# Moving a graph kernel's table look-ups from the node stage into the first softmax and the weighting stage

## The reference

```python
edge_index = jnp.stack([src, dst])
x = _layernorm(x + _L0_gnn_ref(x, node_vec, edge_weight, edge_attr_128, ...))   # attention over incoming edges
x = _layernorm(x + _L1_gnn_ref(x, ...))                                         # three graph convolutions
x = _layernorm(x + _L2_gnn_ref(x, edge_attr_128, src, dst, ...))                # two message layers
x = _layernorm(x + _L3_gnn_ref(x, edge_attr_2, src, dst, ...))                  # edge attention
```

## Time and profile before

| | us |
|---|---|
| timed runs: median (lowest to highest) of 3 | 3603.18 (3602.86 to 3603.41) |
| the profiled execution's own time | 3606.04 |
| its span, first to last instruction | 3604.0 |
| VectorE busy | 2602.9 (72%) |
| TensorE busy | 2523.9 (70%) |
| GpSimd busy | 2052.6 (57%) |
| ScalarE busy | 2013.2 (56%) |
| granted TensorE clock, mean | 0.86 |

### The profile page before, as it was taken

How to read it: one execution, slowest core, us unless ns; L and a number is a source line. 1 busy time by engine, 2 the same in 40 slices (tenths; PEclk the granted TensorE clock), 3 DMA queues, 4 the chain that set the end, 5 groups by cost and what they waited for, 6 DMA issues and landing times. The chain is left out here.

```text
span 3604.0 us, 57246 instructions
## 1 busy us (share of the span) xinstructions
PE 2523.9 (70%) x14627; PEld 1907.0 (53%) x14627; DVE 2602.9 (72%) x7782; ACT 2013.2 (56%) x5963; POOL 2052.6 (57%) x1978
## 2 busy tenths in 40 slices
PE   5377744999476777697687787777767757877430
PEld 2133322666355565575466666555557757776430
DVE  8689963444597899998366677798868759878542
ACT  0034322777222888798466677688867748865110
POOL 7767774774000433342777577577467767710776
PEclk9799986999799988999899899888889979987555
DMA  3455557776299444432566677677589879933221
GB/s 94 106 147 153 154 151 165 248 243 205 86 328 273 141 147 147 135 92 77 174 212 199 190 244 247 217 239 240 181 252 269 241 237 290 284 121 112 86 89 42
DMA packets 521868, 653.93 MB, mean 181 GB/s; under 512 B 99208, under 2 KB 292294, under 8 KB 521544
## 3 DMA queue, kind: packets, MB, share of 16 engines
q1 hardware_dynamic: 455242, 548.98, 48.8%
q0 software_dynamic: 65856, 100.90, 10.3%
q10 hardware_dynamic: 446, 0.40, 0.0%
HBM read 436.87 MB, written 241.92 MB: 188 GB/s over the span
## 5 line engine op out<-in xcount | busy, mean ns | idle before, releaser
L1620 POOL DMA_INDIRECT look<-table_d,ids x196 | 196.1, 1000 | 603.8 <-DVEq L1596 559.7
L1945 POOL DMA_INDIRECT xg_c<-r_d,src_row x392 | 410.9, 1048 | 167.9 <-issue 117.1
L2703 POOL DMA_INDIRECT out<-x_f,out_row x196 | 202.9, 1035 | 177.3 <-DVE x_f L2769 118.5
L1945 POOL DMA_INDIRECT xg_c<-x1d_d,src_row x196 | 216.8, 1106 | 104.8 <-issue 59.5
L1945 POOL DMA_INDIRECT xg_c<-x2d_d,src_row x196 | 203.5, 1038 | 113.0 <-issue 59.2
L925 POOL DMA_INDIRECT xd<-in_x,ids x196 | 217.6, 1110 | 71.0 <-issue 51.7
L1945 POOL DMA_INDIRECT xg_c<-g1d_d,src_row x196 | 204.7, 1044 | 79.6 <-issue 59.5
L554 POOL DMA_INDIRECT rows_d<-row,slot_i x196 | 194.1, 990 | 69.4 <-issue 55.8
L2059 ACT ACTIVATE term_c<-xg_c,scale 128x128 f32<-128x128 f32 x392 | 125.1, 391 | 181.3 <-DMA xg_c<-x1d_d,src_row 107.6
L1964 DVE TENSOR_TENSOR_SCAN agg_t_c<-flags_c,agg_t_c,term_t_c 128x512 f32<-128x512 bf16 x96 | 122.9, 1281 | 104.7 <-ACT term_t_c L2043 59.9
L1964 DVE TENSOR_TENSOR_SCAN agg_t_c<-flags_c,agg_t_c,t_ps_c 128x512 f32<-128x512 bf16 x144 | 183.2, 1273 | 1.0 <-PE t_ps_c L2366 1.0
(11 more groups left out here) (483 smaller groups left out, 8896.0 us busy)
## 6 DMA issues: line engine op xcount, KB each, us to landing
flags_c<-cont_d SPq DMA_DIRECT2D x245, 128.0 KB, 4.4
xm<-rows_d SPq DMA_DIRECT2D x49, 512.0 KB
m_d<-m_c SPq DMA_DIRECT2D x98, 256.0 KB
r_d<-r_c SPq DMA_DIRECT2D x98, 256.0 KB
m_in_c<-m_d SPq DMA_DIRECT2D x98, 256.0 KB
e_c<-rows_d SPq DMA_DIRECT2D x98, 256.0 KB
x_f<-in_x SPq DMA_DIRECT2D x67, 256.0 KB, 4.9
out<-x_f SPq DMA_DIRECT2D x67, 256.0 KB
```

The lines of the kernel that those rows point to most:

```text
L1620: pool.indirect_dma_start(out=look[:, t, :], out_offset=None, in_=table_d[:, :], in_offset=bass.IndirectOffsetOnAxis(ap=ids[:, 0, t:t + 1] ...
L1945: pool.indirect_dma_start(out=xg[:, s, k, :], out_offset=None, in_=table, in_offset=bass.IndirectOffsetOnAxis(ap=src_row[:, t:t + 1], axis=0),
L2703: pool.indirect_dma_start(out=out[:, :], out_offset=bass.IndirectOffsetOnAxis(ap=out_row[:, t:t + 1], axis=0), in_=x4[:, n % SF, k, :], in ...
```

## The change

The 196 look-ups leave the node stage. A function `look_up(pool, begin, end)` issues the look-ups of tiles begin to end one after the other, with no wait between them, and then waits until all so far have landed. GpSimd gets a part in the first softmax that looks up tiles 0 to 49 (FIRST_LOOKS is 50), and one in the weighting stage for tiles 50 to 195 (146 of them). The semaphore `looked` is taken before the first softmax and given back after the weighting stage. The whole diff:

```diff
--- before.py
+++ after.py
@@ -1116,6 +1116,18 @@
 
 
 
+        looked = signal("looked", 16, "pool_queue")
+        FIRST_LOOKS = 50
+
+        def look_up(pool, begin, end):
+
+            for t in range(begin, end):
+                pool.indirect_dma_start(
+                    out=look[:, t, :], out_offset=None, in_=table_d[:, :],
+                    in_offset=bass.IndirectOffsetOnAxis(ap=ids[:, 0, t:t + 1], axis=0),
+                    bounds_check=TABLE - 1, oob_is_err=False).then_inc(looked.sem, 16)
+            pool.wait_ge(looked.sem, looked.at(end))
+
         with ExitStack() as st:
             given_l = sb("given_l", [ROWS, 3, LONG], F32, st)
             most = sb("most", [ROWS, 3, LONG], F32, st)
@@ -1134,6 +1146,10 @@
                     for v in range(2):
                         sp.dma_start(attn_d[v, :].rearrange("(r l) -> r l", l=LONG), seen[:, v, :]).then_inc(once_out.sem, 16)
                     sp.wait_ge(once_out.sem, once_out.at(2))
+
+                @block.gpsimd
+                def _(pool):
+                    look_up(pool, 0, FIRST_LOOKS)
 
                 @block.tensor
                 def _(pe):
@@ -1226,6 +1242,10 @@
                     for s in range(3):
                         sp.wait_ge(x1_out[s].sem, x1_out[s].at(len(range(s, GROUPS, 3))))
 
+                @block.gpsimd
+                def _(pool):
+                    look_up(pool, FIRST_LOOKS, TILES)
+
                 @block.tensor
                 def _(pe):
                     for n in range(GROUPS):
@@ -1286,7 +1306,7 @@
                             settled(dve)
                             dve.tensor_tensor(x1[:, n % 3, :, :], y_ps[n % 3][:, :].rearrange("p (k d) -> p k d", k=K),
                                               inv[:, n % 2, :].unsqueeze(2).to_broadcast([P, K, D]), ALU.mult).then_inc(x1_ready.sem, 1)
-            retire([(s, GROUPS) for s in (weighted, scanned, made_y, squared, x1_ready)])
+            retire([(s, GROUPS) for s in (weighted, scanned, made_y, squared, x1_ready)] + [(looked, TILES)])
             for s in (spread_ready, rooted):
                 s.spent(GROUPS)
             retire([(g_in[s], 5 * shares(s, SG)) for s in range(SG)] + [(x1_out[s], shares(s, 3)) for s in range(3)])
@@ -1328,7 +1348,6 @@
             shift = sb("shift_n", [P, 2, K], F32, st)
             rest = sb("rest_n", [P, K], F32, st)
             setup = signal("dense_setup")
-            looked = signal("looked", 16, "pool_queue")
             x_in = [signal(f"x_in{s}", 16) for s in range(6)]
             x4_out = [signal(f"x4_out{s}", 16) for s in range(3)]
             s_out = [signal(f"s_out{s}", 16) for s in range(2)]
@@ -1612,17 +1631,6 @@
                         sp.wait_ge(x2_out[s].sem, x2_out[s].at(len(range(s, GROUPS, 2))))
                         sp.wait_ge(g1_out[s].sem, g1_out[s].at(len(range(s, GROUPS, 2))))
 
-                @block.gpsimd
-                def _(pool):
-                    for it in range(1, NG):
-                        pool.wait_ge(spread_ok.sem, spread_ok.at(it))
-                        for t in range(TILES * (it - 1) // (NG - 1), TILES * it // (NG - 1)):
-                            pool.indirect_dma_start(
-                                out=look[:, t, :], out_offset=None, in_=table_d[:, :],
-                                in_offset=bass.IndirectOffsetOnAxis(ap=ids[:, 0, t:t + 1], axis=0),
-                                bounds_check=TABLE - 1, oob_is_err=False).then_inc(looked.sem, 16)
-                    pool.wait_ge(looked.sem, looked.at(TILES))
-
                 @block.tensor
                 def _(pe):
                     for it in range(NG + LAG):
@@ -1644,7 +1652,7 @@
 
             retire([(s, NG) for s in (turned_x, xt_ready, made_1, squared_1, y2_ready, turned_y, yt_ready, squared_2, made_2,
                                       g1_ready, made_3, leaked, halved, summed_2, added_u)])
-            retire([(looked, TILES), (setup, 1), (spread_ok, NG + 7), (rooted_n, NG + 7), (inv_ready, NG + 7), (normed, NN)])
+            retire([(setup, 1), (spread_ok, NG + 7), (rooted_n, NG + 7), (inv_ready, NG + 7), (normed, NN)])
             retire([(s, GROUPS) for s in (sloped_g, x1s_ready, x2s_ready, turned_g, g1o_ready)])
             retire([(x_in[s], len(range(s, NG, 6))) for s in range(6)] + [(x4_out[s], len(range(s, NN, 3))) for s in range(3)])
             retire([(group[s], shares(s, 2)) for group in (s_out, x2_out, g1_out) for s in range(2)])
```

## The result

The kernel after takes **3668.5 us** (median of four runs, 3651.4 to 3675.7) against 3603.3 (3602.9 to 3604.3): ratio **1.0174**, 95% interval 1.0143 to 1.0205. I had predicted slower, 3650.7 us in a range of 3638 to 3679; the time lies inside, 17.8 us above my number.

The account below looks back on a forecast made before the run. Each stage was taken to end with its last engine, GpSimd in both filled stages. Node stage 0, softmax +30.0 and weighting stage +17.5 give +47.5 us: 3603.2 becomes 3650.7 us, 8-in-10 range 3638 to 3679.

Parts of the forecast that it names:

- The edge holds GpSimd: At stage edges: GpSimd enters with the other engines, so look-ups of a stage cannot start in the stage before.
- Rival four: At the edges: GpSimd may run on through them, look-ups start before 927, not slower, 3603 us; chance 0.05.
- The node stage is worth 0: Node stage: taking the look-ups out brings 0 us, bounds 0 and -1, as VectorE and ScalarE cover them.
- The price, and what holds a look-up: Per look-up: 1.00 us plus 0.30 of issue; VectorE instructions with both inputs in SBUF hold it until they end.
- Softmax, +30.0: First softmax: 50 look-ups outlast the old stage end and add 30.0 us, bounds +25.9 to +32.0.
- Weighting stage, +17.5: Weighting stage: 146 look-ups, some held by VectorE, end late and add 17.5 us, bounds 0 and +43.
- what SP's last write took: Both stage ends: 1.9 us from the last look-up's end to the next stage's first issue, taken from SP's write.
- Five look-ups in two rounds: Weighting stage: beside VectorE's rounds of 3.63 us, five look-ups take two rounds, 7.25 us, 1.45 us each.
- DMA 0: Weighting stage: DMA traffic of 146 look-ups, 7.2 us, could delay VectorE but stays under GpSimd's tail; 0 us.
- rival one: Weighting stage: only two look-ups a round, 1.81 us each, +43 us there, 3676 us in all; chance 0.20.
- Two (nothing held): Both stages: no look-up is held, softmax +25.9 and weighting stage 0, 3629 us in all; chance 0.09.
- Three: Weighting stage: VectorE waits for look-ups too, 20 to 69 us in place of 17.5, middle 3678 us; chance 0.06.

Follow-up runs that it names:

- the repeat of before: The kernel before, unchanged, run again with a profile on the same chip: 3604.2 us, its weighting stage 189.3 us.
- the split: Against the kernel before: 24 look-ups in the first softmax, 96 in the weighting stage, 76 in the node stage; 3601.4 us against 3601.3, ratio 0.9997.
- weighting only: The change with only its 146 weighting-stage look-ups moved, the other 50 back in the node stage: 3638.7 us, ratio 1.0098 to the kernel before.

## Why the prediction was right, and where its terms were off

*The edge holds GpSimd*: right. The softmax starts at 927.87, its first look-up at 928.57; the weighting stage at 1000.68 and 1001.40. Rival four is out.

*The node stage is worth 0*: right. 555.5 to 558.5 us in five kernels with 50, 76, 146 or no look-ups in it, 556.3 with all 196; the 561.1 of after's profile came in no other.

*The price, and what holds a look-up*: right, and now shown. Two inputs in SBUF hold it; with one in PSUM none of 146 is held.

*Softmax, +30.0*: measured +31.2. That is luck: two errors nearly cancel. From the stage's start to the last look-up's end I had 69.8 us, it was 66.9: 7 are held, but for 1.4 us in all, where I had 4.2 (996.9 less 992.7). The tail was 5.9 us, not 1.9.

*Weighting stage, +17.5*: measured +26.0 (29 to 33 against the repeat of before). The term that was mis-sized is again "what SP's last write took": 5.0, not 1.9, +3.1. It was taken from another engine's work; in its place stand the last look-up's landing (1.5 and 1.9 us at the two edges) and GpSimd's DRAIN (4.1 and 2.7). The stretch without an issue adds 7.1 and was in no step, though before shows two such in its node stage, hidden there, of 5.25 us ahead of its 35th look-up (1249.68) and 3.15 ahead of its 114th (1479.88). Its DRAIN of 6.8 us was in that trace too. The rest came out 1.8 shorter. 17.5 + 3.1 + 7.1 - 1.8 = 25.9.

*Five look-ups in two rounds*: right in kind. "A scan that lets GpSimd pass is 0.05 us longer" was right for the scan, but I did not ask which of VectorE's other operations the next look-up would meet: two rounds are 7.47 us, not 7.25, worth 0.04 us a look-up. The held one takes 1.96 us, not 1.76.

*DMA 0*: right. VectorE's last x is out at 1197.2, 22 us ahead of the stage's end.

*The rivals.* The median, 3668.5, is nearer to rival one's 3676 than to my 3650.7; that it came out so is the tail and the stretch, not the rival's mechanism. The trace decides against that: two look-ups a round would have been 1.81 us each, they came every 1.46 to 1.49. Two (nothing held) fell with the held ones. Three happened on a small scale: VectorE waits for GpSimd, with its 128x4 operations, 5.0 us in all, under GpSimd's tail. The Trainium skill (SBUF — State Buffer, "Who interferes with whom") lists tensor_scalar, not only operations with two SBUF inputs, among those that can take the pair of ports and then contend, if their operands allow it. The trace agrees in that the TENSOR_SCALAR of 128x4 is held (0.40 us for 0.17), and I had weighed the rule for the scan alone. By this section of the Trainium skill whoever issues first keeps the pair for its whole instruction; the traces differ, since a TENSOR_SCALAR that starts in the first 0.50 us of an indirect DMA isn't held.

*The number.* It lies in the range for reasons that were partly not mine: of the 11.4 us between my +47.5 and the profile's +58.9, the two tails are +7.1, the stretch +7.1, fewer or shorter holds -4.7, and the rest lies outside the two stages. The other 6 us up to the median are differences between runs. What is not explained is the spread, 24 us over the change's first four runs where before had 1.4, though on the later chips before spread by 13 and 20 us too.

## What to carry to other kernels

An idle engine offers room only up to the end of the stage's own last worker. Before moving work under it, fill the stage on paper (first start, spacing beside that neighbour, and the engine's own way out of the stage, 5 to 6 us here) and move only what fits: 24 and 96 look-ups fitted and cost nothing where before takes 3601 us, 50 and 146 cost 65. Count in the way out what grows with the work: GpSimd's DRAIN was 7.9 us behind 96 look-ups. On the two chips where before takes 4286 and 4317 us even what fitted cost 56 to 74 us, so measure on more than one. Take the tail from an edge that the same engine reaches last after the same kind of work, not from whichever edge is near. And where work leaves a place in which it was hidden, expect nothing back.

## What the runs showed of the hardware

- The order of the two starts isn't all. A scan with two SBUF inputs that starts 0.06 us ahead of a look-up takes 1.32 us for 1.28, and the look-up passes; a look-up that starts 0.13 us into the scan is held until 0.8 us behind its end. A TENSOR_SCALAR of 128x4 runs freely in the first 0.50 us of an indirect DMA, and one that starts 0.55 to 0.76 us into it ends 0.03 us ahead of its end (130 of 130).
- GpSimd leaves a stage with a DRAIN. Behind k look-ups whose landing it has waited for, it takes 0.04 us and 0.082 for each (20 to 96 of them), and behind 130, 146 and 196 as much as for 113 fewer. It starts some 0.1 us behind the last landing, which comes 1.5 and 1.9 us after the last look-up's end at the change's two edges (6.2 us after the 96th of the split, in the midst of the stage's transfers), and the next stage's first instruction comes 0.24 us behind its end. Without the wait the next stage came 4.4 us (50 look-ups) and 3.5 us (146) behind the last look-up's end.
- A weighting stage with over 113 look-ups has one stretch of 3.1 to 7.4 us in which GpSimd issues nothing, ahead of the 114th, in all eight profiles, and so has the node stage of before, with 196; 50 look-ups fewer ahead of the stage or 32 instructions more don't move it. Why it is 3.1 us once and 7.4 another time is open.
- There are stretches of another kind in the node stage: 5.25 us ahead of the 35th of 196 look-ups (before), 13.87 ahead of the 13th of 50 (weighting only), 6.55 ahead of the 41st of 76 (24 / 96 / 76). The DRAIN behind the 50 and the 76 is as long as for all of them, so these don't begin the count anew. The runs of 132 and 196 indirect DMAs of the earlier trace rows have no such stretch. The cause is open.
- The price of the same change differed by chip: 65 us, and 181 to 194 us.
